# Causal self-attention: the value products of two steps issued together behind every even step

## The reference

```python
K = einsum('bse,hed->bhsd', xk, Wk); V = einsum('bse,hed->bhsd', xv, Wv); Q = einsum('bqe,hed->bhqd', xq, Wq)
scores = einsum('bhqd,bhkd->bhqk', Q, K)
if masked:
    causal = triu(ones((n, n), bool), k=1)
    scores = where(causal, -inf, scores)
att = softmax(scores / sqrt(n), axis=-1)
out = einsum('bhqk,bhkd->bhqd', att, V)
out = out.transpose(0, 2, 1, 3).reshape(b, n, -1)
return relu(out @ Wo + bo)
```

## Time and profile before

| what | value |
|---|---|
| median of 3 runs | 2649.67 us |
| profiled execution, its own time | 2645.53 us |
| its span | 2643.8 us |
| granted clock of PE over the span | 0.961 |
| PE busy | 2394.4 us, 91% |
| DVE, ACT, POOL busy | 61%, 49%, 50% |
| self-attention walk, of the span | 1040 to 1677 us |

### The profile page before, as it was taken

The page is one execution under the profiler, slowest core; times in us unless marked ns, Lnnn a source line. Parts: engine busy times, 40 slices in busy tenths (PEclk is TensorE's granted clock), DMA queues, the critical chain, the costliest instruction groups (busy, mean ns, idle before and its releaser), DMA issues. The chain is left out here.

```text
span 2643.8 us, 42280 instructions
## 1 busy us (share of the span) xinstructions
PE 2394.4 (91%) x12771; PEld 1437.0 (54%) x12787; DVE 1609.2 (61%) x3275; ACT 1298.3 (49%) x2567; POOL 1310.7 (50%) x2112
## 2 busy tenths in 40 slices
PE   6997999999996986899999999899969966999997
PEld 3554786666663553345444453455546653666664
DVE  5885674655554976777868767598866653221221
ACT  4664454444442883566666666567644421222221
POOL 3665773234445652233443535467865214656663
PEclk9998999999998997999999999999989987999999
DMA  4001000000100005131231311010013151322222
GB/s 142 6 1 54 15 0 1 1 1 1 48 1 16 1 1 128 38 91 37 62 89 33 101 49 49 25 33 17 1 34 135 49 201 29 48 45 44 48 44 28
DMA packets 86128, 115.34 MB, mean 44 GB/s; under 512 B 15480, under 2 KB 65536, under 8 KB 84272
## 3 DMA queue, kind: packets, MB, share of 16 engines
q1 hardware_dynamic: 67408, 92.65, 11.7%
q0 software_dynamic: 18528, 20.31, 4.8%
HBM read 78.01 MB, written 34.64 MB: 43 GB/s over the span
## 5 line engine op out<-in xcount | busy, mean ns | idle before, releaser
L3458 ACT ACTIVATE L2S_pT<-L2S_t_ps 128x512 f32<-128x512 f32 (+3 forms) x768 | 356.5, 491 | 221.6 <-PE L2S_t_ps L3279 213.0
L3522 DVE TENSOR_REDUCE L2S_mx<-L2S_s_ps 128x1 f32<-128x768 f32 (+7 forms) x384 | 350.2, 951 | 104.7 <-PE L2S_s_ps L3202 104.1
L3279 PE MATMUL L2S_t_ps<-L2S_q,L2S_k 98*128 98x512 bf16 (+3 forms) x768 | 249.6, 335 | 17.4 <-DMA L2S_q<-L2S_mrow 7.3
L3764 POOL TENSOR_SCALAR_AFFINE_SELECT L2S_pT<-L2S_pT 128x128 f32<-128x128 f32 x512 | 151.2, 310 | 174.0 <-ACT L2S_pT L3458 169.9
L3201 PE MATMUL L2S_s_ps<-L2S_k,L2S_q 96*128 96x512 bf16 (+3 forms) x768 | 200.0, 333 | 11.5 <-DVE L2S_mx L3522 7.6
L622 POOL TENSOR_TENSOR L_prob<-L_prob,L_rc 128x616 f32<-128x616 f32 x64 | 82.2, 1285 | 231.2 <-DVE L_rc L555 231.2
L4140 DVE TENSOR_TENSOR L3B_h<-L3B_si,L3B_u_ps 128x512 f32<-128x512 f32 x71 | 48.8, 688 | 237.0 <-PE L3B_u_ps L4083 237.0
L4057 POOL DMA_INDIRECT out<-L3B_y,L3F_rows x71 | 114.7, 1616 | 134.5 <-DVE L3B_y L4146 122.3
L3279 PEld LDWEIGHTS L2S_t_ps<-L2S_q,L2S_k 98*128 98x128 bf16 x768 | 73.0, 98 | 197.8 <-ACT L2S_pT L3458 128.4
L3379 PE MATMUL L2S_o_ps<-L2S_pT,L2S_v 128*32 128x512 f32 (+3 forms) x1536 | 166.7, 507 | 0.0
L319 PE MATMUL L_scores<-weights,L_xT 128*128 128x308 f32 x512 | 143.1, 423 | 2.3 <-ACT L_xT L442 1.6
(11 more groups left out here) (548 smaller groups left out, 5748.1 us busy)
## 6 DMA issues: line engine op xcount, KB each, us to landing
qk_parts<-L2S_part SPq DMA_DIRECT2D x84, 128.0 KB, 2.3
L2S_q<-qk_parts SPq DMA_DIRECT2D x32, 192.0 KB, 3.4
L2S_k<-qk_parts SPq DMA_DIRECT2D x30, 192.0 KB, 3.4
L2S_q<-qk_parts SPq DMA_DIRECT2D x32, 128.0 KB, 3.2
L3F_w<-in_L_gu SPq DMA_DIRECT2D x8, 512.0 KB, 7.5
weights<-in_L_w SPq DMA_DIRECT2D x8, 512.0 KB, 9.7
out<-x_sb SPq DMA_DIRECT2D x8, 512.0 KB, 4.0
expert_rows<-L_xn SPq DMA_DIRECT2D x8, 512.0 KB, 3.3
```

The source lines that it names most:

```text
L3279: nc.tensor.matmul(o[:, lo:512], k6[:, q % 2, j, kt * P:(kt + 1) * P], q6[:, q % 2, c, j, lo:512], start=True, stop=True).then_inc(s["t_fu ...
L3458: nc.scalar.activation(pT[:, st % SLOTS, j, lo:512], t_ps[j % 2][:, lo:512], ACT.Exp, scale=SK).then_inc(s["exp_done"], 1)
L3522: nc.vector.tensor_reduce(dst, src, AX.X, ALU.max).then_inc(s["mx_done"], 1)
L3764: nc.gpsimd.affine_select(out=edge, in_=edge, compare_op=ALU.is_ge, fill=0.0, base=0, pattern=[[1, P]], channel_multiplier=-1).then_inc(s[ ...
```

## The change

Behind a step of odd number no value products are issued any more. Behind a step of even number st the products of the steps st - 2 and st - 1 are issued, one set behind the other (behind step 0 those of the steps 10 and 11 of the quarter before). The copy of a finished query block follows the second set if that was the block's last, so behind steps 4 and 0 instead of 5 and 1. All engines follow the same walk. The waits inside each set, the closing walk and everything else are as before.

```diff
--- before.py
+++ after.py
@@ -2979,11 +2979,13 @@
                                 project(PROJECT.index(at), j - 1)
                             if at in MAKE_V_NEXT and j in (1, 2):
                                 make_v(MAKE_V_NEXT.index(at), j - 1, False)
-                    done = (q, st - 2) if st > 1 else (q - 1, NS - 2 + st)
-                    if done[0] >= 0 or not first:
-                        values(*done)
-                        if done[1] in (TB // 2 - 1, NS - 1):
-                            copy_out(done[0], STEPS[done[1]][0])
+                    if st % 2 == 0:
+                        of, two = (q, st - 2) if st else (q - 1, NS - 2)
+                        if of >= 0 or not first:
+                            values(of, two)
+                            values(of, two + 1)
+                            if two + 1 in (TB // 2 - 1, NS - 1):
+                                copy_out(of, STEPS[two + 1][0])
 
         def last_walk(values=nothing, copy_out=nothing, turn_out=nothing, spread=nothing):
```

## The result

The change takes 2661.38 us, the median of five runs from 2660.32 to 2668.82; the kernel before, timed beside it, 2649.67 us (2645.51 to 2651.04). The ratio is 1.0055, with an interval of 1.0038 to 1.0072: 11.7 us slower, where 9 were forecast. The profiled run of the change is the slowest of its five, 2668.82 us, and the one of before one of its fastest, 2645.53 us. So the two traces lie 23.3 us apart, twice what the medians do; 17.8 us of that are in the attention walk and 5.5 ahead of it and behind it, where nothing was changed.

A forecast was written before the change was run, and what follows sets the result against it. PE, busy 607 of 637 us in the attention walk, was taken as close to the bound, coupled to ACT and DVE by two-bank rings. +7.2 us for 14 quarters and +1 for each end gave +9, 2658.7 us; range 2640 to 2670.

The forecast's parts named there:

- The saving at the joins: Value products joined in pairs: 94 entries and exits less, 0.10 + 0.145 us each, 23.0 us of PE time.
- rival 1: Whole kernel: PE is the bound, the placed waits do not come, full 23.0 us saved, 2626.7 us; chance 16%.
- The walk of the plain quarter: Quarter holding only attention: 23.06 to 25.16 us without value blocks, exits give back 0.87, net +1.2 on 32.50.
- Steps 3 and 4, said to be bound by DVE: Attention-only quarter: DVE sets the pair's end, so without the value block between it goes from 3.82 to 4.61 us.
- 0.3 to 0.6 that were said to show it: Sign of the forecast: the first score product of an even step waits 0.3 to 0.6 us for ACT.
- The mask: Step 1's masks by POOL are done 0.2 to 0.3 us before the block's second half starts; cost nothing.
- Rival 3: POOL's second mask in step 1 comes 0.6 us later: 4.5 us on top of the forecast, 2663; chance 5%.
- The filled quarters: Pairs whose odd step holds projections or output products: these fill the hole, a gain of 0.1 to 0.2 us.
- Rival 2: Waits come, but ten quarters with other work gain 0.5 us more, the ends 2 more: about +2, 2652; chance 22%.
- The last quarter: Last quarter of the attention walk: no maxima, the ACT ring the bound, put at +1 us.
- The first quarter: First quarter of the attention walk: three reductions in each late step, DVE the bound, put at +1 us.
- The forecast case: Whole kernel: the uncovered waits outweigh the saved entries and exits, +9 us, 2658.7 on the median; chance 57%.

## Why the prediction was right, point by point

**The saving at the joins: right.** 0.245 us a join was read from rows of before. Taking the joins apart gave 0.25 each where PE is the bound. The Trainium skill, "TensorEngine Tiling (Array Packing)", Key Properties, says that a change of tiling mode drains the engine. The 0.25 us of each extra switch agree with it. The saving alone would have made the kernel 23 us faster: rival 1 did not come.

**The walk of the plain quarter: right.** Pairs of steps with their value blocks, in us; the change's blocks put behind the lengths that the prediction walked:

| pair | before | walk | change |
|---|---|---|---|
| (1,2) | 4.95 | 5.68 | 5.61 |
| (3,4) | 5.18 | 5.40 | 5.40 |
| (5,6) | 5.89 | 6.32 | 6.36 |
| (7,8) | 6.89 | 6.73 | 6.74 |
| (9,10) | 5.41 | 5.73 | 5.73 |
| (11,0) | 4.17 | 3.86 | 3.95 |
| quarter | 32.50 | 33.7 | 33.81 |

The pairs hold different blocks before and after, so only their sum can be compared between the first and the last column. In steps 9 and 10 the walk also had the two starts right, 2.23 us for step 10's first score product and 4.09 for the block (1651.10 and 1652.96 against 1648.87). Steps 3 and 4, said to be bound by DVE, end as the walk had it. PE at their seam:

```profile
1631.59 0.28 PE L3281 MATMUL L2S_t_ps<-L2S_q,L2S_k 98*128 98x128 bf16 x2
1632.27 0.38 PE L3281 MATMUL L2S_t_ps<-L2S_q,L2S_k 98*128 98x512 bf16 x1 [0.40 <-ACT L2S_pT L3460]
...
1633.59 0.45 PE L3203 MATMUL L2S_s_ps<-L2S_k,L2S_q 96*128 96x512 bf16 x2 [0.33 <-DVE L2S_mx L3524]
```

The first score product of the even step waits 0.40 us for ACT, and 0.32 at step 10, inside the 0.3 to 0.6 that were said to show it. It is 0.20 at step 2, and at steps 6 and 8 the profile names none, though the product starts 0.06 us behind its exponential there. The idle named before both kinds of products grew by 16.9 and 5.2 us, 15 or more together.

**The mask: right.** POOL and PE at the end of step 2 of the plain quarter:

```profile
1627.83 0.98 POOL L3719 DMA_DIRECT2D L2S_q<-L2S_mrow  x2 [1.13 <-DVE L2S_mrow L3530]
1628.81 1.51 POOL L3766 TENSOR_SCALAR_AFFINE_SELECT L2S_pT<-L2S_pT 128x128 f32<-128x128 f32 x6
```

```profile
1628.71 1.71 PE L3381 MATMUL L2S_o_ps<-L2S_pT,L2S_v 128*32 128x512 f32 x16
```

The second mask behind the DMAs, the last that the block's second half needs, ends at about 1629.3; that half starts at 1629.56. The second half starts 0.88 us behind the first in every quarter from the third of batch 0 to the last but one. In the second quarter of batch 0 it is 1.10 to 1.15, the only one at full clock that may have waited. The 0.3 us for which value products wait for POOL by the page stand at the very end of the walk, before the block of step 11. Rival 3 did not come.

**The filled quarters: mis-sized, in both directions.** "Filled pairs at -0.1 to -0.2" was too good. In the first quarter of batch 3 steps 5 and 6 went from 7.92 to 8.77 us, their blocks from 1.35 to 1.86, so the rest grew by 0.34 and the pair by 0.2 after its saved exit. The projections stand at the second and third unit, and the wait at a seam falls on the first. The whole quarter went +0.4 where the terms give -0.45, and the third quarters of batches 1 and 2 +1.2 where they give +0.4.

The terms can be held against the traces one by one. This is each kind of pair over the 14 quarters, change less before at full clock, with the value columns taken out. Each step is taken from the profile in which it is shorter, and the dip of before in batch 2 is taken off. In us:

| pairs | (1,2) | (3,4) | (5,6) | (7,8) | (9,10) | (11,0) | sum |
|---|---|---|---|---|---|---|---|
| forecast | +4.2 | +6.5 | -2.8 | -2.1 | +1.8 | -0.4 | +7.2 |
| traces | +3.2 | +5.2 | +0.6 | -5.8 | +3.8 | +2.0 | +9.0 |

In the plain quarters every pair is within about 0.1 us of its term. What is off are the pairs next to other work.

Rival 2 named what runs the other way, and it exists. In the second quarter of batches 1 and 2 of before, PE stands in step 7 because DVE is late with its splits and norms. Batch 1:

```profile
1279.84 0.28 PE L3212 MATMUL L2S_r_ps<-ident,L2S_mx 128*16 128x128 f32 x1 [2.07 <-DVE weights L3538]
```

```profile
1276.79 1.38 DVE L3652 TENSOR_SCALAR weights<-weights,L2S_mv_y,L2S_rs_y 128x256 f32<-128x256 f32 x4
1278.08 1.08 DVE L3522 TENSOR_REDUCE L2S_mx<-L2S_s_ps 128x1 f32<-128x896 f32 x1
...
1279.36 0.42 DVE L3538 TENSOR_TENSOR weights<-L2S_r_ps,L2S_rc 128x256 f32<-128x256 f32 x1
```

and in the change, with the block of step 5 already done behind step 6:

```profile
1286.53 0.28 PE L3214 MATMUL L2S_r_ps<-ident,L2S_mx 128*16 128x128 f32 x1 [1.21 <-DVE weights L3540]
```

The wait is shorter by 0.86 us there, and step 7 with it (5.84 to 3.89, of which 1.00 is the block that moved out of it). With 1, 7 and 11 moved and 5 left, step 7 stays at 5.84. A smaller wait of this kind, 0.5 to 0.6 us in step 7 of four more quarters of before, went as well: their pairs (7,8) gained 0.4 to 0.5 us more than counted. So rival 2's mechanism is at work in six quarters of sixteen and gave about 3.5 us, against the 5 in ten quarters that it was priced at.

The second quarter gained 0.7 us in batch 1 and 2.4 in batch 2. The 1.6 us between are the clock, not the rings. In before the lower level comes right behind this stall in batch 2, and the next block takes 1.62 us to the score product behind it instead of 1.00:

```profile
1442.51 0.28 PE L3212 MATMUL L2S_r_ps<-ident,L2S_mx 128*16 128x128 f32 x1 [2.06 <-DVE weights L3538]
1442.71 1.68 PE L3379 MATMUL L2S_o_ps<-L2S_pT,L2S_v 128*32 128x512 f32 x8
```

In the traces that keep a stall of 1.8 to 2.1 us here (before twice, 1, 7 and 11 moved, before's order with half the work) six of eight such quarters have a stretch of 3.4 us at the lower level behind it. In the nine other traces, where it is 0.9 to 1.2 us, one of eighteen has. So the change, by moving step 5's block, most likely also saves a dip now and then, 1.6 us each; the prediction had nothing of that.

The errors cancel only in part. For the 14 quarters 7.2 us were forecast, and 9.0 to 9.4 came at full clock, or about 7.5 with the dip that before has. Seen quarter by quarter, the sum is right by luck as much as by its terms.

**The last quarter: mis-sized, and the largest miss.** +1 was put down, +7.5 and +5.0 came. The term missed the clock, and was small even without it. The last quarter has no maxima, and PE is busy 29.69 us of its 34.50 in before. The granted clock of a window gives the time at the lower of the two levels, 1.2 GHz: at a mean of 0.72 it is 0.28 x 2 = 0.56 of 42.04, 23.5 us; in the second profile 13.5; in before 3.4 both times. A joined block then takes twice as long, here the one behind step 6 of the last quarter of the change:

```profile
1676.87 3.64 PE L3381 MATMUL L2S_o_ps<-L2S_pT,L2S_v 128*32 128x512 f32 x16
1680.44 0.61 PE L3281 MATMUL L2S_t_ps<-L2S_q,L2S_k 98*128 98x512 bf16 x1
```

3.57 us against 1.86 in the plain quarter. From the change's own two profiles, (42.04 - 39.68) / (23.5 - 13.5) = 0.24 us for each us at the lower level; carried to before's 3.4, the quarter would take some 37.3, +2.8. That is an estimate from two points. Other runs bear on it. The run with the last quarter in before's order spent 16.9 us at the lower level and took 38.38 us, where the same line puts the change's order at 40.5: 2.1 more for the order at an equal clock. And the two kernels with half the work have a mean of 1.00 there and take 29.76 and 31.42 us, +1.7. So the order costs 1.7 to 2.8 us, and the clock the rest. Why the lower level lasts longer under the change is open. It is not the order of the last quarter's own products alone, since that was before's in a run with a mean of 0.78 and in one with 1.00.

**The first quarter: right.** +1 was put down, and like clocks give +1.0 to +1.5. What the prediction says of the quarters, from 32.50 to 42.81 us, leaves this one out: it takes 54.02 us in before, at a mean clock of 0.81. The second quarter of batch 2, at 44.37, is outside too.

**The sum.** The forecast case came: 2661.4 against 2658.7, its own range 2652 to 2668. At like clocks the parts, +1.0 to +1.5, +9.0 to +9.4 and +1.7 to +2.8, add up to some 12 to 14 us for the walk, or 10 to 12 with the dip that before has. That is 1 to 3 us over the forecast of 9, and the medians are 11.7 us apart. What the profiles show on top is the clock of single executions. The three fastest of the change's five runs (2660.32 to 2661.38 us, the median among them) had a mean granted clock of 0.961 or 0.962 over the whole execution, and the profiled one had 0.956. That the last quarter of the median run was shorter than 42.04 us is likely, but not shown, since only the profiled execution has a trace.

## What to carry to other kernels

A block of work on the bounding engine that needs neither partner's result is what hides their latency; before bunching it to save switches, walk the ring of banks over the seam that it leaves, with the durations of the rows. Bunch only at seams where something else already covers the wait or where the engine stands anyway: here three joins a quarter made the kernel 0.2% faster and three others 0.6% slower. Judge such an edit by a stretch that repeats to the hundredth, and look at the granted clock before reading anything into a stretch that does not. And take what a wait costs from start to start, not from the idle time that the profile names.

## What was not expected of the hardware

The clock in the sparse last quarter. It stands at the lower level for 0 to 24 us, depending on the kernel and also on the run of one program: 23.5 and 13.5 us for the change, 3.4 and 3.4 for before, none where 2, 5 and 9 are moved ahead of an unaltered last quarter. The quarter's length goes from 33.06 to 42.04 us with it. What starts or ends it was not found. In two quarters elsewhere it came right behind a stall of PE of 1.8 to 2.1 us in six cases of eight, and behind one of 0.9 to 1.2 us in one of eighteen. The other is how much of a bank's turn is not the exponential: of 1.07 us from a score product of 512 columns to the next into the same bank, 0.48 are the way to ACT and back. Half the columns take 0.22 us off the other 0.60.
